# Linear-attention and FP4 feed-forward block: transposing the normalised x by DMA, and splitting the first residual addition over ScalarE and GpSimd

## What is computed

```
xn  = layernorm(x)
q, k, v = split(xn @ W_qkv.T)                # 16 heads of 16
q   = softmax(q) * 16**-0.5 ; k = exp(k)     # softmax over a head's 16
ctx = running sum over earlier 64-row buckets of k.T @ v    # den likewise, of k
att = (q @ ctx) / max(den, 1e-6)             # a bucket sees earlier buckets only
y1  = att @ W_out.T
h   = silu(fp4(xn) @ fp4(Wg).T) * (fp4(xn) @ fp4(Wu).T)     # 704 wide
y2  = fp4(h) @ fp4(Wd).T
out = x + y1 + y2
```

## Time and profile before

| | |
|---|---|
| Median of three runs | 1378.86 us |
| The profiled execution: its time, and its span | 1378.78 us, 1377.1 us |
| TensorE busy, VectorE busy | 1301.7 us (95%), 1294.4 us (94%) |
| ScalarE busy, GpSimd busy | 1028.2 us (75%), 250.1 us (18%) |
| DMA engines, share of the span | 39.6% for the one busy queue |
| Mean granted TensorE clock | 0.989 of full speed |

### The profile page before, as it was taken

The page is one execution under the profiler, slowest core; times in us unless marked ns, Lnnn a source line. Parts: engine busy times, 40 slices in busy tenths (PEclk is TensorE's granted clock), DMA queues, the critical chain, the costliest instruction groups (busy, mean ns, idle before and its releaser), DMA issues.

```text
span 1377.1 us, 41687 instructions
## 1 busy us (share of the span) xinstructions
PE 1301.7 (95%) x10318; PEld 913.1 (66%) x10318; DVE 1294.4 (94%) x3901; ACT 1028.2 (75%) x3349; POOL 250.1 (18%) x664
## 2 busy tenths in 40 slices
PE   0279999999999999999999999999999999999996
PEld 0257676677767677676767677676766767676674
DVE  6769999999999999999999999999999999999996
ACT  1577778777787878777787877778787777878772
POOL 2211212111121211112121111112111111212110
PEclk9889999999999999999999999999999999999998
DMA  4023444444344444334444433434444343434334
GB/s 124 4 38 64 91 89 84 88 93 87 78 102 87 84 89 95 83 80 95 92 85 88 97 83 81 99 85 84 88 98 89 76 96 85 92 81 99 81 69 89
DMA packets 362747, 116.85 MB, mean 85 GB/s; under 512 B 327772, under 2 KB 362204, under 8 KB 362716
## 3 DMA queue, kind: packets, MB, share of 16 engines
q1 hardware_dynamic: 361990, 115.80, 39.6%
q10 hardware_dynamic: 726, 0.72, 0.2%
HBM read 19.99 MB, written 16.78 MB: 27 GB/s over the span
## 4 chain that ended last, share of the span: by engine, by line
PE 92%; DVE 4%; ACT 1%; issue 1%; DMA 1%; SPq 0%; DVEq 0%; ACTq 0%
PE outp L1168 11%; PE nump L1118 6%; PE unit1a L1058 6%; PE unit0a L1058 6%; PE outp L1170 5%; PE unit1a L1060 5%; PE unit1a L1062 5%; PE unit0a L1060 5%; PE unit0a L1062 5%; PE ctxp L1128 4%; PE unit1b L1058 4%; PE unit1b L1060 4%; PE unit1b L1062 4%; PE unit0b L1058 4%; PE unit0b L1060 4%; PE unit0b L1062 4%
## 5 line engine op out<-in xcount | busy, mean ns | idle before, releaser
L1168 PE MATMUL outp<-w_down_cat,q_rows 128*128 128x256 f16 x1408 | 246.0, 274 | 0.0
L599 ACT ACTIVATE snap<-ctxp,mask 64x68 f32<-64x68 f32 x1024 | 236.1, 308 | 3.2
L409 POOL TENSOR_TENSOR var_scaled<-squares,var_mul 128x1 f32<-128x1 f32 x128 | 33.5, 262 | 947.8 <-ACT scratch L492 947.8
L1168 PEld LDWEIGHTS outp<-w_down_cat,q_rows 128*128 128x128 f16 x1408 | 138.3, 98 | 16.5
L1170 PE MATMUL outp<-w_down_lo,q_rows 128*128 128x256 f16 x640 | 147.6, 274 | 0.0
L517 ACT ACTIVATE xnt<-trp 128x256 f16<-128x256 f32 x256 | 97.3, 380 | 58.5 <-PE trp L1082 58.5
L562 ACT ACTIVATE th<-unit1a,c_g 128x352 f32<-128x352 f32 x128 | 70.9, 554 | 83.8 <-PE unit1b L1062 83.8
L562 ACT ACTIVATE th<-unit0a,c_g 128x352 f32<-128x352 f32 x128 | 71.0, 555 | 83.0 <-PE unit0b L1062 81.8
L810 DVE TENSOR_REDUCE blk<-h 128x44 f32<-128x704 f32 x128 | 123.8, 967 | 0.1
L863 DVE TENSOR_TENSOR hx_v<-h,blk 128x704 f32<-128x704 f32 x128 | 112.1, 876 | 0.0
L400 POOL TENSOR_TENSOR att_s<-att,att_s 128x256 f16<-128x256 f32 x128 | 86.5, 676 | 124.2 <-ACT att_s L554 124.2
(11 more groups left out here) (203 smaller groups left out, 4156.4 us busy)
## 6 DMA issues: line engine op xcount, KB each, us to landing
xring<-x SPq DMA_DIRECT2D x128, 128.0 KB, 2.7
out<-xring SPq DMA_DIRECT2D x128, 128.0 KB, 2.5
xqt<-xq_s SPq DMA_TRANSPOSE x128, 2.4
att_t<-att_s SPq DMA_TRANSPOSE x128, 2.5
q_rows<-q_rows SPq DMA_TRANSPOSE x128, 3.6
raw_qkv<-wqkv_t SPq DMA_DIRECT2D x1, 768.0 KB, 4.3
raw_up<-wup ACTq DMA_DIRECT2D x2, 352.0 KB
raw_gate<-wgate SPq DMA_DIRECT2D x2, 352.0 KB
```

What stands on the lines that cost most here:

```text
L599: nc.scalar.activation(kept[:, :, cols], sums[:, :, cols], ACT.Copy, scale=mask[rows, f, h:h + 1])\
L1168: nc.tensor.matmul(downp, hqt[:, par, m, :], w_down_cat[:, m, :], start=(m == 0), stop=False)
```

## The change

The transposition of the normalised x leaves TensorE. ScalarE now rounds the untransposed xn of tile k+3 to its float16 high half (`high_xn`, behind `mean_of`), GpSimd subtracts to get the low half (`low_xn`), and SyncE issues a transposing DMA of both halves (`turn_xn`), which `project_qkv` waits for. `transpose_xn`, `less_xn`, `split_xnt` and the matrix `minus16` go. The first part of `add_up` leaves VectorE: ScalarE scales `attp` out of PSUM into a new buffer `att_o` (`scale_att`, behind `exp_k`), and GpSimd adds x (`add_x`, first in its step, ahead of `low_att`). One `add_up` remains on VectorE, and it waits for `x_added`; `o_step` counts once a tile. `transpose_q` and `gate_up` lose their place between the parts that left.

```
 # SyncE
+            def turn_xn(t, par):
+                sp.wait_ge(xn_lo, after(t))
+                if begun(t - 2):
+                    sp.wait_ge(qkv_done, after(t - 2))
+                sp.dma_start_transpose(xnt[...], xn_s[...]).then_inc(xn_turned[par], 16)
...
                     turn_h(2 * i + d - 1, 1 - d)
+                    turn_xn(2 * i + d + 3, 1 - d)
 # GpSimd
+            def low_xn(t, par):
+                pool.wait_ge(xn_hi, after(t))
+                nc.gpsimd.tensor_tensor(xn_s[:, par, 1, :], xn[:, par, :], xn_s[:, par, 0, :], ALU.subtract).then_inc(xn_lo, 1)
+            def add_x(n, d):
+                pool.wait_ge(att_scaled, after(t))
+                if begun(t - 2):
+                    pool.wait_ge(o_step, after(t - 2))
+                nc.gpsimd.tensor_tensor(osum[:, d % 2, :], att_o[:, :], xring[...], ALU.add).then_inc(x_added, 1)
...
             def step(n, d):
+                add_x(n, d - 3)
                 low_att(k - 1, odd)
+                low_xn(k + 3, odd)
                 rstd_of(k + 4, par)
 # ScalarE
+            def high_xn(t, par):
+                act.wait_ge(xn_done, after(t))
+                if begun(t - 2):
+                    act.wait_ge(xn_turned[par], turned(t - 2, par))
+                nc.scalar.activation(xn_s[:, par, 0, :], xn[:, par, :], ACT.Copy).then_inc(xn_hi, 1)
+            def scale_att(t):
+                act.wait_ge(proj_done, after(t))
+                if begun(t - 1):
+                    act.wait_ge(x_added, after(t - 1))
+                nc.scalar.activation(att_o[:, :], attp, ACT.Copy, scale=c_o[:, :]).then_inc(att_scaled, 1)
...
                 exp_k(k + 1, odd)
+                scale_att(k - 3)
                 exp_q(k + 1, odd)
...
-                split_xnt(k + 2, par, 0)
                 normalise_waits(k + 3)
                 mean_waits(n, d + 4)
-                split_xnt(k + 2, par, 1)
...
                 mean_of(n, d + 4)
+                high_xn(k + 3, odd)
 # VectorE
                 round_hx(k - 1, k + 2, 0)
-                add_up(n, d - 3, 0)
                 round_hx(k - 1, k + 2, 1)
-                add_up(n, d - 3, 1)
+                add_up(n, d - 3)
 # TensorE
             def project_qkv(t, par):
-                pe.wait_ge(xnt_split, after(t, 2))
+                pe.wait_ge(xn_turned[par], turned(t, par))
...
                 gate_up(k, 0, par)
-                transpose_xn(k + 2, par)
-                gate_up(k, 1, par, (0,))
-                less_xn(k + 2, par)
-                gate_up(k, 1, par, (1,))
+                gate_up(k, 1, par)
                 transpose_q(k + 1, odd)
```

More of the change, by code:

```diff
@@ L109, in linear_attention_fp4_ffn_block @@
         ident16 = sb("ident16", [P, P], fp16)
-        minus16 = sb("minus16", [P, P], fp16)
         mask = sb("mask", [P, 2, HH])
@@ L126, in linear_attention_fp4_ffn_block @@
         xn = sb("xn", [P, 2, D])
+        xn_s = sb("xn_s", [P, 2, 2, D], fp16)
         xnt = sb("xnt", [P, 2, 2, D], fp16)
@@ L159, in linear_attention_fp4_ffn_block @@
         osum = sb("osum", [P, 2, D])
+        att_o = sb("att_o", [P, D])
         unit = [[pb("unit0a"), pb("unit0b")], [pb("unit1a"), pb("unit1b")]]
@@ L177, in linear_attention_fp4_ffn_block @@
         consts = sem("consts")
-        minus_ready = sem("minus_ready")
         w_max = sem("w_max")
@@ L191, in linear_attention_fp4_ffn_block @@
         xn_done = sem("xn_done")
-        xnt_tr = sem("xnt_tr")
-        xnt_split = sem("xnt_split")
-        xnt_less = sem("xnt_less")
+        xn_hi = sem("xn_hi")
+        xn_lo = sem("xn_lo")
+        xn_turned = [sem(f"xn_turned{par}") for par in range(2)]
         qkv_done = sem("qkv_done")
@@ L226, in linear_attention_fp4_ffn_block @@
         o_step = sem("o_step")
+        att_scaled = sem("att_scaled")
+        x_added = sem("x_added")
         x_dram = x.rearrange("(q s n t p) d -> q n s p t d", s=2, t=2, p=BUCKET, n=SEQ_TILES // 2)
@@ L288, in store @@
                 sp.sem_inc(sp_turn, 1)
-                sp.wait_ge(o_step, (i + 1) * 4)
+                sp.wait_ge(o_step, (i + 1) * 2)
                 sp.sem_inc(sp_turn, 1)
@@ L324, in turn_att @@
                                        att_s[:, par, :, :].rearrange("p s k -> p (s k)")).then_inc(att_turned[par], 16)
+            def turn_xn(t, par):
+                if not is_tile(t):
+                    return
+                sp.wait_ge(xn_lo, after(t))
+                sp.sem_inc(sp_turn, 1)
+                if begun(t - 2):
+                    sp.wait_ge(qkv_done, after(t - 2))
+                sp.sem_inc(sp_turn, 1)
+                sp.dma_start_transpose(xnt[:, par, :, :].rearrange("p s (c k) -> p (s c) k", k=P),
+                                       xn_s[:, par, :, :].rearrange("p s k -> p (s k)")).then_inc(xn_turned[par], 16)
             def turn(i):
@@ L341, in _ @@
                 load(0, n)
+            turn_xn(0, 0)
             turn(-1)
@@ L390, in _ @@
             pool.wait_ge(consts, 3)
-            nc.gpsimd.tensor_tensor(minus16[:, :], zeros16[:, 0:P], ident16[:, :], ALU.subtract).then_inc(minus_ready, 1)
             for g in range(HG):
@@ L401, in low_att @@
                     .then_inc(att_lo, 1)
+            def low_xn(t, par):
+                if not is_tile(t):
+                    return
+                pool.wait_ge(xn_hi, after(t))
+                nc.gpsimd.tensor_tensor(xn_s[:, par, 1, :], xn[:, par, :], xn_s[:, par, 0, :], ALU.subtract).then_inc(xn_lo, 1)
+            def add_x(n, d):
+                t = 2 * n + d
+                if not is_tile(t):
+                    return
+                pool.wait_ge(att_scaled, after(t))
+                if begun(t - 2):
+                    pool.wait_ge(o_step, after(t - 2))
+                nc.gpsimd.tensor_tensor(osum[:, d % 2, :], att_o[:, :], xring[:, (n + d // 2) % XCH, d % 2, :], ALU.add)\
+                    .then_inc(x_added, 1)
             def rstd_of(t, par):
@@ L500, in normalise_waits @@
                 if begun(t - 2):
-                    act.wait_ge(xnt_tr, after(t - 2))
+                    act.wait_ge(xn_lo, after(t - 2))
                 if begun(t - 2):
@@ L509, in normalise @@
                                      bias=shift[:, d % 2, :], scale=rstd[:, d % 2, :]).then_inc(xn_done, 1)
-            def split_xnt(t, par, part):
+            def high_xn(t, par):
                 if not is_tile(t):
                     return
[L514 to L517, removed]
+                act.wait_ge(xn_done, after(t))
+                if begun(t - 2):
+                    act.wait_ge(xn_turned[par], turned(t - 2, par))
+                nc.scalar.activation(xn_s[:, par, 0, :], xn[:, par, :], ACT.Copy).then_inc(xn_hi, 1)
             def exp_k(t, par):
@@ L576, in factor_of_row @@
                 if begun(t - 2):
-                    act.wait_ge(o_step, after(t - 2, 2))
+                    act.wait_ge(o_step, after(t - 2))
                 nc.scalar.activation(c_row[:, par, :], hrow[:, 1, :], ACT.Copy, scale=c_d[:, :]).then_inc(c_row_done, 1)
@@ L930, in low_scales, with add_up @@
                                                    ALU.subtract).then_inc(hq_step, 1)
-            def add_up(n, d, part):
+            def add_up(n, d):
                 t = 2 * n + d
@@ L936, in add_up @@
                 here = xring[:, (n + d // 2) % XCH, d % 2, :]
[L937 to L947, removed]
+                dve.wait_ge(x_added, after(t))
+                dve.wait_ge(c_row_done, after(t))
+                nc.vector.scalar_tensor_tensor(here, downp, c_row[:, d % 2, :], osum[:, d % 2, :], ALU.mult, ALU.add)\
+                    .then_inc(o_step, 1)
             def step(n, d):
@@ L1049, in _ @@
             pe.wait_ge(consts, 7)
-            pe.wait_ge(minus_ready, 1)
             def clear_context():
@@ L1063, in three_passes @@
                 return end
[L1065 to L1083, removed]
             def project_qkv(t, par):
@@ L1101, in transpose_q @@
                 pe.wait_ge(q_exp, after(t))
-                pe.wait_ge(xnt_split, after(t + 1, 2))
+                if begun(t - 1):
+                    pe.wait_ge(qt_done, after(t - 1))
                 for c in range(KC):
@@ L1157, in project_att @@
                 if begun(t - 1):
-                    pe.wait_ge(o_step, after(t - 1, 2))
+                    pe.wait_ge(o_step, after(t - 1))
                 for c in range(KC):
```

## The result

The changed kernel takes 1436.59 us, the median of four runs (1434.03 to 1437.52), against 1379.03 us (1377.84 to 1380.28) for the one before: ratio 1.0414, 95% interval 1.0396 to 1.0432. It is 4.1% slower, on the forecast side of no change and inside the stated range, near its upper end; the forecast was 1415 us.

What follows compares the result with a forecast made beforehand. TensorE set the pace, VectorE a quarter of a microsecond behind. VectorE's 9.52 + 0.8 = 10.32 us against 10.04 gave +35 us over about 125 steps, plus 1.3 us, on 1378.78 us: 1415 us, range 1336 to 1440.

Steps and rivals of the forecast that it cites:

- TensorE saves 0.36 us, no gain of its own: TensorE loses two transpositions and a subtraction, 0.34 to 0.39 us a step; alone it would then need 9.68 us.
- The snapshot: ScalarE's snapshot of the context, next that could be late for TensorE: slack 0.38 us, at worst 0.1 us a step.
- VectorE saves 0.27 us by L941: L941 goes from VectorE, so L892 could start at 604.68 instead of 604.95; own work becomes 9.52 us a step.
- Two collisions, 0.8 us, of 0.5 to 1.0: On VectorE, add_x costs L863 (now L903) 0.33 us and low_att costs L870 (now L910) about 0.5 us a step.
- D: The end of add_up on VectorE, 605.75 us in the profile before, from which the forecast counted add_x's start.
- full lock: GpSimd and two-SBUF-input VectorE operations exclude each other for whole instructions: second collision 0.67 us, 0.95 us together.
- The sum: VectorE's 9.52 + 0.8 = 10.32 us a step against 10.04 before; +35 us over about 125 steps.
- The 1.3 us for the tail: In the last two tiles nothing covers the longer way through ScalarE and GpSimd: +0.65 us each.
- SyncE at no cost: Two more transposing issues, 3 us a pair, fit SyncE's idle 5.3 us; otherwise up to 0.5 us a step.
- `low_xn` at no cost: On GpSimd it falls where VectorE mostly multiplies out of PSUM; between 0 and 0.5 us, 0 was taken.
- Rival B: No loss on VectorE: GpSimd finds gaps or waits, TensorE's 9.68 us sets the pace, 1335 us; chance 0.20.
- Rival C: One collision only, about 0.5 us, add_x being through before L863 (now L903): 10.02 us a step, 1378 us; chance 0.15.

Runs made afterwards that it cites:

- wait_last: The changed kernel with the three waits ahead of L932 reordered, the wait for the first rounding now last: 1411.77 us.
- xn_alone: The changed kernel with only the DMA transposition of xn; add_up in two parts on VectorE, scale_att and add_x gone: 1361.77 us.
- early_wait_last: scale_early with the waits ahead of L932 reordered as in wait_last: 1347.15 us, ratio 0.9781 to the kernel before.
- low_att_first: The changed kernel with the first two operations of GpSimd's step exchanged, low_att ahead of add_x: 1398.39 us.
- scale_early: low_att_first with scale_att ahead of exp_k on ScalarE and add_x's wait for att_scaled last of its two: 1361.25 us.

## Why the prediction was right, and where its sizes were off

- *TensorE and VectorE share the bound, with a quarter of a microsecond between them.* Right, and slightly low: VectorE could have started the maximum over q some 0.1 us before the end of the operation ahead of it, so its own work was 9.70 us and not 9.79.
- *TensorE saves 0.36 us, no gain of its own.* TensorE now waits 0.58 to 0.75 us a step for `add_up`, at `project_att` as predicted. The snapshot, named as next in line, did not hold anything up in the steady steps.
- *VectorE saves 0.27 us by L941.* This term was mis-sized. L941 had covered not only its own work but VectorE's handling of the three waits ahead of L932. Without it 0.20 to 0.24 us of that lie bare, so the instruction's removal was worth some 0.05 us. wait_last measured what lies bare: 25 us in all.
- *Two collisions, 0.8 us, of 0.5 to 1.0.* The mechanism and the number of collisions were right; the places were not those of the forecast (L903 and L910) but those of its upper end: L903 came first and was left whole, and L910 and L924 paid, 0.54 us and 0.35 us, 0.89 us together. That a single-input operation can be the one that pays had no price in the sum. `add_x` reached GpSimd 613.79 - 606.84 = 6.95 us after D instead of 6.5 us, the sum of `scale_att`'s 0.47 us for an expected 0.38 (0.09 us more; exp_k, which also reads PSUM and takes its scale from a tensor, has 0.47 us as well, and would have been the better row), a handover of 0.31 us for 0.07, and a start on ScalarE 0.12 us later than worked out; L903 came 613.45 - 606.84 = 6.61 us after D, 0.11 us earlier. Why `low_att` costs L924 only 0.35 us can be read from the rows. L910 stands there from 0.08 us before the end of L903 (603.79 against 603.87), L924 only from 0.04 us behind the end of L910 (604.78 against 604.74), which makes 0.12 us; and counted from the end of the VectorE operation ahead of it, `low_att` takes 605.27 - 604.74 = 0.53 us where `add_x` takes 604.46 - 603.87 = 0.59. No run varies this. The prediction's sum by a full lock should read 0.33 + 0.67 = 1.00 us, not 0.95; nothing hangs on it.
- *The sum.* 9.70 - 0.05 + 0.89 = 10.54 us against a measured 10.51; the prediction's 9.52 + 0.8 = 10.32 lacks the 0.2 us of bare waits. Those 0.2 us are 25 us over 125 steps, and the time missed is 1436.59 - 1415 = 22 us, so the mis-sized saving is the whole error. The other two deviations, VectorE's own work (-0.09 us) and the collisions (+0.09 us), cancel, and that is luck. The 1.3 us for the tail can't be told from the noise.
- *SyncE at no cost, `low_xn` at no cost.* Both right. xn_alone bears out the first, the rows of L421 and L945 the second.
- *Rival B* (TensorE's 9.68 us) did not hold; it is about what early_wait_last reaches with the same operations in other places. *Rival C*, one collision, is low_att_first. It came out at 1398 us and not 1378, by the same bare waits.
- The two signs named beforehand were these: L903 near 1.2 us or L910 near 0.9 us, and TensorE waiting for `add_up`. L910 came out at 0.95 us, and TensorE does wait there.

## What to carry to other kernels

Moving work to an idle GpSimd is not free because GpSimd is idle. Where its operation reads SBUF while VectorE runs a product of two SBUF tensors or a fast scalar operation, one of them stands still; for a VectorE operation that comes second the price here was 0.35 to 0.53 us for 256 columns, and it is paid again for a GpSimd operation that is queued behind and pushed into the same stretch. Look at what VectorE runs at the moment of the handover, and move the operation beside reductions or operations fed from PSUM: here two exchanged lines gave back 38 us and an earlier start another 37.

When a removed instruction stood between two dependent ones, read the gap that it covered before booking its duration, and put the wait that is met last behind the others: worth 0.2 us a step here.

## What the runs showed of the hardware beyond that

- A GpSimd operation waiting behind a VectorE operation gets in ahead of VectorE's next one, in every step; one that arrives as a VectorE operation starts waits for that whole one (L421 at 608.50 against L945 at 608.53), and it costs nothing where the operations behind are not of the kind that is stopped.
- A two-input product is stopped by a GpSimd operation that reads (0.53 us for 256 columns, 0.26 us for 128), and not by a memset that only writes (side by side for 0.35 us, neither longer).
- Scalar operations of 16 and 44 columns are stopped too: in scale_early L866 took 405 ns on average against 166 ns, and in xn_alone L847 took 333 ns against 265.
- By the rows shown, a stopped L910, L924 or L930 goes on 0.14 to 0.16 us before the recorded end of the GpSimd operation that stops it.
- Three waits ahead of an instruction cost 0.2 us when the first of them is met last, and some 0.03 us when the last is. On GpSimd the same exchange of two waits was worth 0.07 us, and a register operation ahead of an instruction addressed by the loop's counter took 0.10 us.
